# Third stage of a four-block kernel: three side banks, a new order of the side work, and the output sums moved to GpSimd

## What is computed

```python
h = norm_scale * x / (nrm + EPS) * split_scale
q = (h @ Wq.T).reshape(b, s, H, dh)           # H = 8 heads
k = (h @ Wk.T).reshape(b, s, G, dh)           # G = 2 groups
v = (h @ Wv.T).reshape(b, s, G, dh)
scores = jnp.einsum('bghsd,bgtd->bghst', q, k) / np.float32(np.sqrt(dh))
attn = jax.nn.softmax(scores, axis=-1)
out = jnp.einsum('bghst,bgtd->bghsd', attn, v)   # then heads side by side
return x + out @ Wo.T
```

## Time and profile before

| | |
|---|---|
| median of the runs | 1461.83 us |
| the profiled execution, its own time | 1460.45 us |
| its span, first to last instruction | 1458.6 us |
| third stage, first score to last score matmul | 320 to 929 us |
| one middle batch of it | 76.5 us |
| granted TensorE clock over the span | 0.989 of full |

### The profile page before, as it was taken

How to read it: one execution, slowest core, us unless ns; L and a number is a source line. 1 busy time by engine, 2 the same in 40 slices (tenths; PEclk the granted TensorE clock), 3 DMA queues, 4 the chain that set the end, 5 groups by cost and what they waited for, 6 DMA issues and landing times.

```text
span 1458.6 us, 20717 instructions
## 1 busy us (share of the span) xinstructions
PE 1386.4 (95%) x6864; PEld 1134.4 (78%) x6864; DVE 1010.8 (69%) x2070; ACT 798.1 (55%) x1554; POOL 740.7 (51%) x1008
## 2 busy tenths in 40 slices
PE   5999999988999999999999999799999999999996
PEld 4888877766777877878787887588888888888884
DVE  5888869867989898989898989666242442434333
ACT  4666646647777878786868788632222222213221
POOL 5888646735536465554646455553343424333241
PEclk9999999999999999999999999999999999999998
DMA  6665133241302112121212041430101011010100
GB/s 192 169 174 127 40 101 116 87 130 38 94 4 64 65 44 88 44 87 37 87 28 96 15 121 40 145 138 1 58 1 59 4 54 58 0 58 0 58 29 29
DMA packets 53516, 101.32 MB, mean 69 GB/s; under 512 B 3760, under 2 KB 4784, under 8 KB 53424
## 3 DMA queue, kind: packets, MB, share of 16 engines
q1 hardware_dynamic: 49728, 92.83, 19.1%
q0 software_dynamic: 3696, 7.34, 3.1%
HBM read 70.79 MB, written 25.17 MB: 66 GB/s over the span
## 4 chain that ended last, share of the span: by engine, by line
PE 75%; DVE 13%; POOL 4%; issue 4%; ACT 3%; DMA 1%; SPq 0%; POOLq 0%; DVEq 0%; ACTq 0%
PE context L1889 13%; PE score L2367 11%; PE context L2367 11%; PE context L58 6%; PE score L58 6%; PE context L2395 5%; PE turned L2395 5%; PE score L899 4%; PE turned L1925 4%; PE context L1951 2%; PE context L1953 2%; DVE g_neg_max L1754 2%; PE context L1925 2%; DVE g_q L1677 1%; DVE g_ptl L1770 1%
## 5 line engine op out<-in xcount | busy, mean ns | idle before, releaser
L1413 POOL TENSOR_SCALAR g_prob<-g_prob,g_inv_sum 128x512 f32<-128x512 f32 x256 | 178.0, 697 | 268.9 <-DVE g_inv_sum L1759 268.8
L1548 ACT ACTIVATE g_prob<-score,g_neg_max 128x512 f32<-128x512 f32 x256 | 177.2, 692 | 115.5 <-DVE g_neg_max L1754 113.1
L2143 POOL TENSOR_TENSOR f_hl<-f_hidden,f_hh 128x512 fp32r<-128x512 f32 x88 | 121.9, 1386 | 216.0 <-DVE f_hh L2276 216.0
L1754 DVE TENSOR_REDUCE g_neg_max<-score 128x1 f32<-128x512 f32 x256 | 174.7, 682 | 43.9 <-PE score L58 43.4
L2367 PE MATMUL context<-g_hth,f_w 128*128 128x512 f32 x352 | 137.8, 391 | 2.3 <-ACT f_w L2193 2.2
L2367 PE MATMUL score<-g_hth,f_w 128*128 128x512 f32 x352 | 137.8, 392 | 0.6 <-DVE g_htl L2293 0.5
L2367 PE MATMUL context<-g_htl,f_w 128*128 128x512 f32 x352 | 137.1, 390 | 0.0
L2367 PE MATMUL score<-g_htl,f_w 128*128 128x512 f32 x352 | 137.1, 390 | 0.0
L58 PE MATMUL score<-g_kh,g_q 128*128 128x512 f32 x256 | 123.4, 482 | 10.7 <-ACT g_prob L1548 7.5
L2199 ACT ACTIVATE f_silu<-score,g_bits 128x512 f32<-128x512 f32 x44 | 30.3, 690 | 176.1 <-PE score L2367 176.1
L2199 ACT ACTIVATE f_silu<-context,g_bits 128x512 f32<-128x512 f32 x44 | 30.4, 690 | 174.5 <-PE context L2367 174.5
(11 more groups left out here) (261 smaller groups left out, 3950.6 us busy)
## 6 DMA issues: line engine op xcount, KB each, us to landing
xt<-x_t SPq DMA_DIRECT2D x16, 512.0 KB, 6.9
x_mixed<-x_resident SPq DMA_DIRECT2D x8, 1024.0 KB, 4.4
x_pair<-x_mixed SPq DMA_DIRECT2D x8, 1024.0 KB, 8.2
g_res<-x_mixed SPq DMA_DIRECT2D x8, 1024.0 KB, 6.5
x_attended<-g_res SPq DMA_DIRECT2D x8, 1024.0 KB, 5.1
x_pair<-x_attended SPq DMA_DIRECT2D x8, 1024.0 KB, 5.6
x_resident<-x SPq DMA_DIRECT2D x7, 1024.0 KB, 11.3
factor_sum<-factors POOLq DMA_DIRECT2D x7, 1024.0 KB, 10.8
```

The lines of the kernel that those rows point to most:

```text
L1413: nc.gpsimd.tensor_scalar(prob[:, at, :], prob[:, at, :], inv_sum[:, at:at + 1], 1.0, ALU.mult, ALU.mult).then_inc(prob_ready, 1)
L1548: nc.scalar.activation(prob[:, at, :], score[u % 2][:, :], ACT.Exp, bias=neg_max[:, at:at + 1], scale=1.0, accum_out=row_sum[:, at:at + 1] ...
L1754: nc.vector.reduce_max(neg_max[:, at:at + 1], score[u % 2][:, :], AX, negate=True).then_inc(max_ready, 1)
L2143: self.nc.gpsimd.tensor_tensor(self.hl[:, at, :], self.hidden[:, at, :], self.hh[:, at, :].bitcast(F32), ALU.subtract).then_inc(self.hl_re ...
```

## The change

- Side work: the order of the items is another, the planner's share is 6, 5 or 3 in place of 8, 7 or 3, and the items go over three banks. The third is the bank that the transposes give up; these have two, so unit u waits for the low part of unit u - 2.
- The statistics, the scale steps `H` and the two first `CONVERT` steps move by one or two steps.
- ScalarE copies both halves of a finished head (`parts_of`), and this frees the bank. GpSimd adds them for a pair of heads at once (`sum_of`, steps 15, 23, 31 and 39, the last being step 7 of the next batch), casts the sum and subtracts the low part (steps 26, 27, 32 and 39).
- VectorE makes the reciprocals of two units in one instruction in every even step; GpSimd then normalises both. VectorE has neither sums nor casts of the output any more.
- At the end the fourth stage has its banks by other names.

```diff
-SUM_LAG = OUT_LAG + 2
+SUM_AT = tuple(OUT_LAG + T + 2 + 2 * T * m for m in range(T))
-NAMES = ["v", "q1", "q2", "q3", "h0", "h1", "wo0", "wo1", "h2", "h3", "wo2", "k", "wo3", "q0", "vt"]
+NAMES = ["q1", "v", "q2", "q3", "h0", "wo0", "h1", "wo1", "h2", "wo2", "h3", "wo3", "k", "q0", "vt"]
-H = (5, 6, 8, 11)
-CONVERT = (25, 26, 32, 39)
-SHARE, SHARE_AT_END, SHARE_BESIDE_OUT = 8, 7, 3
+H = (5, 6, 9, 13)
+CONVERT = (26, 27, 32, 39)
+SHARE, SHARE_AT_END, SHARE_BESIDE_OUT = 6, 5, 3
...
+def side_bank(use):
+    return use % 2 if use < AHEAD else 2 - (use - AHEAD) % 3
...
-        score, side, output = s.score, s.side, s.output[0]
-        turned = [s.turned[0], s.turned[1], s.output[1]]
+        score, side, output = s.score, [s.side[0], s.side[1], s.output[1]], s.output[0]
+        turned = s.turned
...
+            def sum_of(b, m):
+                pool.wait_ge(part_ready, b * HEADS + 2 * m + 2)
+                pool.wait_ge(ol_ready, b * T + m + 1)
+                nc.gpsimd.tensor_tensor(out_sum[:, m, :], out_parts[:, 0, :], out_parts[:, 1, :],
+                                        ALU.add).then_inc(sum_ready, 1)
+            def hi_of_output(b, m):
+                pool.wait_ge(sum_ready, b * T + m + 1)
...
+                nc.gpsimd.tensor_copy(oh[:, m, :], out_sum[:, m, :]).then_inc(oh_ready, 1)
...
-                if u > 0 or not first:
-                    if not drain or u == 0:
-                        normalise(b * UNITS + u - 1, u + 3)
+                if u % 2 == 0 and (u > 0 or not first):
+                    normalise(b * UNITS + u - 2, u + 2)
+                    normalise(b * UNITS + u - 1, u + 3)
...
-            def v_lo_of(head, hd):
-                act.wait_ge(out_ready, head + 1)
-                nc.scalar.copy(v_lo_part[:, hd % 2, :], output[HALF[1], :]).then_inc(part_ready, 1)
+            def parts_of(b, hd):
+                if hd % 2 == 0 and b + hd > 0:
+                    act.wait_ge(sum_ready, b * T + hd // 2)
+                act.wait_ge(out_ready, b * HEADS + hd + 1)
+                for part, half in enumerate(HALF):
+                    last = nc.scalar.copy(out_parts[HALF[hd % 2], part, :], output[half, :])
+                last.then_inc(part_ready, 1)
...
-                    nc.vector.reciprocal(inv_sum[:, at:at + 1], row_sum[:, at:at + 1]).then_inc(inv_ready, 1)
+                    nc.vector.reciprocal(inv_sum[:, at:at + 2], row_sum[:, at:at + 2]).then_inc(inv_ready, 2)
...
+            def side_bank_free(b, use):
+                if use == AHEAD:
+                    pe.wait_ge(rest.mixed_ready, B * T)
+                elif use > AHEAD and b < B:
+                    pe.wait_ge(side_free, use - 2)
...
-                        pe.wait_ge(lo_ready, g - TURN_LAG - 2)
+                        pe.wait_ge(lo_ready, g - TURN_LAG - 1)
...
-                            pe.wait_ge(sum_ready, b * HEADS + hd)
+                            pe.wait_ge(part_ready, b * HEADS + hd)
```

More of the change, by code:

```diff
@@ L1075 @@
 SHARES, END = side_schedule()
-AHEAD = len(SPLIT) - len(OWN)
+PROLOGUE = [name for name in SPLIT if name not in OWN]
+AHEAD = len(PROLOGUE)
 WO = [END[f"wo{t}"] for t in range(T)]
@@ L1280, in mixed_bank @@
         def mixed_bank(b, use):
-            return (turned if b == B - 1 else side)[use % 2]
+            return turned[use % 2] if b == B - 1 else side[side_bank(use)]
         @block.sync
@@ L1762, in step @@
                         lo_of(b, p, name, 0 if name == "q0" else None)
-                if u == END["q0"] + 3 and side_runs("q0", first, last, drain):
-                    lo_of(b, p, "q0", 1)
                 turn_u = u - TURN_LAG
@@ L1847, in turn_h @@
                     cols = slice(k * P, (k + 1) * P)
-                    last = nc.tensor.transpose(side[use % 2][:, cols], h[:, t % 2, cols], s.identity[:, :])
+                    last = nc.tensor.transpose(side[side_bank(use)][:, cols], h[:, t % 2, cols], s.identity[:, :])
                 last.then_inc(side_ready, 1)
             def turn_v(b, use):
-                side_bank(use)
+                side_bank_free(b, use)
                 pe.wait_ge(side_hi, side_split(b - 1, "vt"))
@@ L1855, in turn_v @@
                     cols = slice(t * P, (t + 1) * P)
-                    last = nc.tensor.transpose(side[use % 2][:, cols], v_turned[:, cols], s.identity[:, :])
+                    last = nc.tensor.transpose(side[side_bank(use)][:, cols], v_turned[:, cols], s.identity[:, :])
                 last.then_inc(side_ready, 1)
@@ L1865, in side_share @@
                 use = side_use(b, name)
-                out = mixed_bank(b - 1, use) if name[0] == "w" else side[use % 2]
+                out = mixed_bank(b - 1, use) if name[0] == "w" else side[side_bank(use)]
                 if name[0] == "h":
@@ L2050, in __init__ @@
         self.x, self.xth, self.xtl = s.x_pair, g.hth, g.htl
-        first = side_use(B - 1, "wo2") % 2
-        self.inner = [s.side[first], s.side[1 - first], s.score[0], s.score[1]]
-        self.down = [s.output[0], s.output[1], s.turned[0], s.turned[1]]
+        side = [s.side[0], s.side[1], s.output[1]]
+        last = side_use(B - 1, "wo3")
+        self.inner = [side[side_bank(last - 1)], side[side_bank(last)], s.score[0], s.score[1]]
+        self.down = [s.output[0], side[side_bank(last - 2)], s.turned[0], s.turned[1]]
         self.bn, self.mv, self.ve, self.rs, self.shift = norm_in.bn, norm_in.mv, norm_in.ve, norm_in.rs, norm_in.shift
```

88 lines of the change are left out of this document (39 added, 49 removed).

## The result

The changed kernel takes 1468.49 us (median of 6 runs, 1467.02 to 1470.98), the kernel before 1461.87 (6 runs): a ratio of 1.0045, with a 95% interval from 1.0032 to 1.0058. It is slower by 0.45%, where 0.5% faster was forecast. The profiled execution took 1467.02, its span 1465.2.

A forecast was written before the change was run, and what follows sets the result against it. TensorE was taken to bound the kernel. From 1460.45: -21.0 removed waits, +14.3 new waits, -2.5 first batch, +1.7 +0.3 +0.4 last: -6.8, 1453.6; median 1455. Forecast 1450 to 1458.8 (chance 0.42), range 1445 to 1466.

The forecast's parts named there:

- the floor: Middle batch on TensorE: 73.5 us of work without waits, of 76.55 taken, so 3.0 us lost.
- What the new order removes: Three side banks end TensorE's waits: 3.0 us in each of seven batches after the first, 21 us.
- rival D: Side items wait for input, not bank: 3.0 becomes 2.0, result 1462; chance 0.25 together with the no-change rival.
- None of it is on TensorE's path in a middle batch, so I count it at nothing there. It pays for the second bank of transposes that is gone: VectorE's relief, sums of 5.4 us a batch plus casts and reciprocals, counted at nothing in a middle batch.
- The seam on GpSimd: Between batches, GpSimd's chain from step 26 makes TensorE wait: 1.5 us each, plus 0.45 in six seams.
- the 0.3 forecast for step 30: TensorE's wait in step 30 for unit 26's normalisation, ready at 9.3 plus 0.2, wanted at 9.2.
- rival A: GpSimd late at every seam if the cast takes 1.34: 1472, deciding from about 1.1; chance 0.15.
- The other waits: TensorE's new waits a batch: step 0 0.5, step 2 0.7, step 4 0.45, step 9 0.15 us.
- The sum: All terms together: -6.8 us against the profiled 1460.45, giving 1453.6; median 1455.
- the first batch: No output projection there, so VectorE's lighter load counts: gain 2.5 us, between -1 and 5.
- the last batch: Losses of 1.7 in steps 21 to 25, 0.3 in steps 30 and 0, 0.4 before wo0.
- The sum behind the last batch: GpSimd's last sum after 943.5; if locked out by VectorE until 945.3, wo0 comes 0.2 us later.

The follow-up runs named there:

- e10: Changed kernel with GpSimd's seam order changed, reciprocals and normalisations singly, and unit 26's low part ahead of q0's in step 30: 1457.6 us, ratio 0.9973.
- e13: Changed kernel with the outputs' sums and casts put back as before, the last low part ahead of step 8's normalisation pair: 1473.8 us, ratio 1.0090.
- e12: Kernel before the change with VectorE's 25 weight reads cut to 8 of 512 columns: 1457.9 us, ratio 0.9981.
- e5: Changed kernel with VectorE's 25 reads of the next stage's weights cut to 8 of 512 columns: 1460.6 us, ratio 1.0001.
- e4: Kernel before the change with the transposes of the probabilities on two banks instead of three, the third idle: 1463.1 us, ratio 1.0021.
- e8: Kernel before the change with both output halves copied by ScalarE, and sum, cast and low part by pairs of heads on GpSimd: 1468.0 us, ratio 1.0055.
- e1: Changed kernel with the pairing undone, one reciprocal and one normalisation per step: 1467.9 us, ratio 1.0052.
- e2: Changed kernel with VectorE's statistics moved from steps 22 and 24 to 26 and 28: 1470.3 us, ratio 1.0069.
- e6: Changed kernel with unit 26's low part ahead of q0's in VectorE's step 30: 1468.9 us, ratio 1.0055.

## Why the prediction was wrong

**What bounds the kernel, and the floor: right.** 73.5 us were laid out for a middle batch without waits. Batch 4 with its 3.4 us of waits taken off is 73.9. The 0.4 between them is in no wait; in six batches it makes 2.4 us.

**What the new order removes: right.** None of the waits for v's bank, an exponential, h's low part or wo's is left; rival D is out. e10 reaches 75.0 with the same three side banks.

**"None of it is on TensorE's path in a middle batch, so I count it at nothing there. It pays for the second bank of transposes that is gone": this step failed.** VectorE's slack was read from a mean, 69.61 busy of 76.55, and that put its lateness in steps 20 to 30 at nothing. There the statistics, totals, reads and k's low part stand close together and VectorE runs almost without a gap. What the runs showed in its place: TensorE waits 10.1 us in six batches for `g_ptl`, 1.7 a batch, where the sum had 0.65 (0.5 in step 0 and 0.15 in step 9), and GpSimd's chain starts late behind a late reciprocal. Of the 10 us that VectorE gives up only some 2.5 stood in those steps (three sums, two casts), so they don't pay for the bank. Nor are they worth nothing: taking them back costs 4.6 us (e13). Before, a third bank and slack at every normalisation hid the lateness (in batch 4 the tightest, in step 31, ends 1.7 us ahead of its transposes; e12: the reads cost 0.2 us in six batches). In the changed kernel those of steps 30, 2 and 4 end 0.05 us ahead, and e5, which takes 0.6 us three or four times a batch from VectorE, gives 6.3 us back. That it is the loss of both together which exposes VectorE is argued and not shown: in the old order the bank alone costs 2.4 us in six batches (e4) and the sums alone 5.1 (e8).

**The seam on GpSimd: the mechanism right, its start wrong.** From the pair of step 26 to unit 26's normalisation I had 6.6 us of work; it is 693.28 to 699.77, 6.5. But I let it start 1.96 us after the step, from a quiet step 6, and it starts 3.01 after it. This one number, 1.05, is more than the difference between the 0.3 forecast for step 30 and the 1.09 that came; the rest of the chain was some 0.25 shorter. The costs themselves held: cast 0.615 for 0.7, sum 1.29 for 1.34. So rival A's end came in part, by another door: its condition, a cast over 1.1, did not hold.

**The other waits.** Step 2 took 0.32 for 0.7 and step 4 0.43 for 0.45, since step 30 and step 0 had already waited longer. Step 0 took 0.84 and up to 1.84 for 0.5, step 9 0.58 for 0.15; steps 25 and 27 (0.15 and 0.46) were not in the sum at all. Together 3.4 to 5.0 a batch for 2.1.

**The sum.** Over batches 1 to 6 I had 0.9 less in each, 5.4, and it is 7.65 more: 13.05 of a miss of 13.4 (6.6 for -6.8). The rest nearly cancels: the first batch gained 0.5 for 2.5, and in it h0 still waits for its scales (4.25, and 3.65 in the earlier trace rows); the last batch with all behind it came out 0.1 shorter, where its terms and its share of the seven batches gave 1.05 more; the stages ahead took 0.4 less. That these ends nearly cancel is luck: the last batch has 2.4 more in it, most of which goes with the granted clock, and what lies behind it has 2.5 less.

**The sum behind the last batch.** The Trainium skill's page SBUF — State Buffer (Who interferes with whom) was weighed for it. It ran in 1.29 us from 951.35, when VectorE's weight row of 1.76 us at 949.15 was over, since ScalarE's copies came that late. So this trace neither bears the rule out nor goes against it.

**Left open.** What decides how long the granted clock stays low in the last batch, and whether fewer than 25 reads, reads at their old steps, or reads placed in an earlier stage, would bring e10 to 74 us in batches 1 to 3 too. This wasn't tried.

## What to carry to other kernels

An engine with spare time on average can be the late one in the stretch that matters; before costing its relief or its lateness at nothing, lay out its instructions step by step there, and take the start of a chain from the step in question, never from a quiet one. When one edit after another only moves a wait (e1, e2, e6), the waits are links of one chain through several engines: try them together. And a buffer that is taken away is paid for by the slack of everything that it decoupled, not only by the instruction that fills it.
